# Two linear-attention stages: where queries and outputs are transposed, and when the next batch's q and k are made

## The reference

```
# layer 0: 16 heads of 8, causal linear attention
h = layernorm(x) * (1 + ca) + sa
q, k, v = split(h @ w_attn);  q = elu(q) + 1;  k = elu(k) + 1
S_t = S_(t-1) + k_t v_t^T;  z_t = z_(t-1) + k_t
y_t = (q_t S_t) / (q_t z_t + 1e-6);  x = x + ga * (y @ w_proj)
# layer 1: retention, the same sums with a decay per head
q, k = rope(h @ Wq.T), rope(h @ Wk.T);  v = h @ Wv.T
out = ((q k^T * scale) * decay_causal) v
out = groupnorm_per_head(out) * gn_w + gn_b
x = x + ga * ((silu(h @ Wg.T) * out) @ Wo.T)
```

## Time and profile before

| | us |
|---|---|
| median of 3 runs (1055.17 to 1057.34) | 1056.55 |
| the profiled execution | 1054.64 |
| its span, first to last instruction | 1052.8 |
| TensorE busy in the span | 860.5 (82%) |
| VectorE busy | 829.7 (79%) |
| GpSimd busy | 711.0 (68%) |
| ScalarE busy | 609.6 (58%) |

### The profile page before, as it was taken

How to read it: one execution, slowest core, us unless ns; L and a number is a source line. 1 busy time by engine, 2 the same in 40 slices (tenths; PEclk the granted TensorE clock), 3 DMA queues, 4 the chain that set the end, 5 groups by cost and what they waited for, 6 DMA issues and landing times. The chain is left out here.

```text
span 1052.8 us, 24355 instructions
## 1 busy us (share of the span) xinstructions
PE 860.5 (82%) x5240; PEld 622.6 (59%) x5240; DVE 829.7 (79%) x2581; ACT 609.6 (58%) x1524; POOL 711.0 (68%) x450
## 2 busy tenths in 40 slices
PE   5699999999968977888898988639888731999993
PEld 5456666666645754555555655426656521999993
DVE  5468888888875994888888888767988770899995
ACT  2545555555427965565656566347765212999992
POOL 4478878878853535999999999645599562255554
PEclk9799999999987998999999999859999855999997
DMA  8520000000000000000000000064566654544420
GB/s 243 165 66 2 0 0 0 0 0 0 0 1 5 0 1 1 11 11 20 10 20 10 20 10 20 21 184 109 149 207 208 192 193 143 159 131 134 133 68 20
DMA packets 64934, 70.11 MB, mean 67 GB/s; under 512 B 8965, under 2 KB 52178, under 8 KB 64740
## 3 DMA queue, kind: packets, MB, share of 16 engines
q1 hardware_dynamic: 50612, 47.20, 16.2%
q0 software_dynamic: 6368, 16.89, 4.7%
q10 hardware_dynamic: 7872, 5.08, 1.7%
HBM read 32.32 MB, written 24.50 MB: 54 GB/s over the span
## 5 line engine op out<-in xcount | busy, mean ns | idle before, releaser
L475 POOL TENSOR_TENSOR a_kv<-a_qk,a_vv 128x2304 f32<-128x2304 f32 (+1 forms) x64 | 252.0, 3938 | 37.1 <-DVE a_qk L446 32.6
L485 PE MATMUL a_pS<-a_kv,utri 128*128 128x360 f32 (+3 forms) x768 | 259.7, 475 | 10.7 <-POOL a_kv L475 10.7
L574 DVE TENSOR_TENSOR a_tt<-a_pS,a_qk 128x360 f32<-128x360 f32 (+3 forms) x384 | 201.5, 527 | 75.4 <-PE a_pS L485 75.2
L485 PEld LDWEIGHTS a_pS<-a_kv,utri 128*128 128x128 f32 x768 | 140.5, 191 | 96.2 <-issue 29.8
L591 POOL TENSOR_TENSOR a_tt<-a_tt 128x1152 f32<-128x1152 f32 (+1 forms) x64 | 144.7, 2260 | 37.7 <-DVE a_tt L574 37.6
L2016 POOL DMA_INDIRECT out_dram<-x_o,x_place x71 | 69.1, 974 | 76.1 <-DVE x_o L2003 75.1
L602 DVE TENSOR_REDUCE a_nd<-a_tt 128x144 f32<-128x720 f32 (+3 forms) x128 | 104.3, 817 | 1.0 <-POOL a_tt L591 0.9
L538 ACT ACTIVATE a_tt<-a_pI 128x144 f32<-128x144 f32 (+1 forms) x96 | 39.8, 415 | 96.0 <-PE a_pI L493 95.9
L1596 POOL DMA_INDIRECT ys<-m_S,m_dest x64 | 63.0, 984 | 35.2 <-issue 12.7
L546 ACT ACTIVATE a_qT<-a_pQ 128x128 f32<-128x128 f32 x96 | 26.5, 276 | 98.9 <-PE a_pQ L410 83.3
L1954 PE MATMUL x_pZ<-w,x_hT 128*128 x568 | 75.9, 277 | 1.4 <-issue 1.4
(11 more groups left out here) (299 smaller groups left out, 2103.4 us busy)
## 6 DMA issues: line engine op xcount, KB each, us to landing
x_yl<-ys SPq DMA_DIRECT2D x71, 193.5 KB, 2.4
X<-xs SPq DMA_DIRECT2D x16, 256.0 KB, 5.3
kx<-m_kc SPq DMA_DIRECT2D x64, 64.0 KB
ax<-m_pc SPq DMA_DIRECT2D x64, 64.0 KB
m_S<-X SPq DMA_DIRECT2D x16, 256.0 KB, 3.6
xs<-X SPq DMA_DIRECT2D x15, 256.0 KB
w<-in_L_ffn_W_dram SPq DMA_DIRECT2D x1, 2048.0 KB
m_S<-gw ACTq DMA_DIRECT2D x6, 256.0 KB, 2.9
```

Of the source, the lines that this page charges most:

```text
L475: pool.tensor_tensor(kv[:, t:t + 2, :, :, :].rearrange("p t h j i -> p (t h) j i"), kk.unsqueeze(2).to_broadcast([P, 2 * H, J, D]), rows.u ...
L485: pe.matmul(pS[c][:, 0:(h1 - h0) * SC], K.utri[:, :], flat[:, h0 * SC:h1 * SC], start=True, stop=True).then_inc(u_done, 1)
L574: v.tensor_tensor(tt[:, t, h0:h1, :, 0:D], pS[c][:, 0:(h1 - h0) * SC].rearrange("p (h j i) -> p h j i", i=D, j=J), q[:, h0:h1, :].unsqueez ...
```

## The change

1. The q transpose moves from pQ into bank pI, between the inter product and y's transposes. It no longer waits for pQ, but for every reader of pI: the inter copy, the q copy, the y copy.
2. TensorE's step: qkv of ta comes right behind the state sum, ahead of the projection; in layer 0 y is transposed one tile at a time, the first ahead of the q transpose in the middle of the step and the second at the step's end; in layer 1 both at the step's end. The second q transpose stands behind them, at the very end.
3. VectorE's step: q and k of the next batch's even tile (L446, L452 to L457) move ahead of the odd tile's products; the residual moves behind the state.
4. ScalarE's step: the copies out of qkv come ahead of the q copy, and normalise moves behind them, to the end of its half of the step; the second y copy stands behind it, and in layer 1 the gate behind that.
5. GpSimd's step in layer 1: the gate product is done a step later, ahead of rope and kv.

The ScalarE order at the end of layer 0's odd step in the loop, before: `a_yT` is the copy of y, `a_tt` the inter copy, `a_xn` normalise, `a_vv`, `a_ea`, `a_eb` the three operations behind a qkv, and the branch closes the loop.

Normalise and the y copy, which was in the odd step, now stand between the q copy and the gate. The diff, cut to the operations that move:

```diff
@@ places in PSUM and the q transpose
-        YT = H * J
-        QT = 3 * P
+        QT = H * J
+        YT = QT + P
         def pe_transpose_q(pe, b, t):
-            pe.wait_ge(v_ready, m)
             pe.wait_ge(qk_ready, qk_count(b, t))
-            pe.wait_ge(qk_free, m)
+            wait(pe, inter_ready, 3 * b + t - 1)
             wait(pe, qT_ready, 3 * b + t - 1)
-            pe.transpose(pQ[:, QT:QT + P], qk[:, 0, t, :], K.ident[:, :]).then_inc(q_T, 1)
+            wait(pe, yT_read, y_issued(b, t - 1))
+            pe.transpose(pI[:, QT:QT + P], qk[:, 0, t, :], K.ident[:, :]).then_inc(q_T, 1)
@@ pe_step
-            if out:
-                pe_project(pe, *out)
             if cur:
                 if ta > 0:
                     pe_inter(pe, b, ta)
                 pe_state_sum(pe, b, ta)
-                pe_transpose_q(pe, b, ta + 1)
                 if known(b, 1):
                     pe_qkv(pe, b + 1, ta)
-            if back:
-                pe_transpose_y(pe, back, b, u)
+            if out:
+                pe_project(pe, *out)
+            if cur and layer == 1 and u == 0 and known(b, 1):
+                pe_gate(pe, b + 1)
+            if back and layer == 0:
+                pe_transpose_y(pe, back, b, ta)
             if cur:
+                pe_transpose_q(pe, b, ta + 1)
                 pe_states(pe, b, tb)
                 pe_inter(pe, b, tb)
                 if tb < 3:
                     pe_state_sum(pe, b, tb)
-                    pe_transpose_q(pe, b, tb + 1)
                 if known(b, 1):
                     pe_qkv(pe, b + 1, tb)
                 if u == 1 and known(b, 2):
                     pe_transpose_x(pe, b + 2)
+            if back:
+                pe_transpose_y(pe, back, b, tb)
+            if cur and tb < 3:
+                pe_transpose_q(pe, b, tb + 1)
@@ act_step, second half
             if cur:
                 act_inter(act, b, tb)
-                if more:
-                    act_normalise(act, b + 2, tb)
             if layer == 1 and last:
                 act_sd(act, *last)
             if cur:
+                if known(b, 1):
+                    act_qkv(act, b + 1, tb)
                 if tb < 3:
                     act_qT(act, b, tb + 1)
-                if known(b, 1):
-                    act_qkv(act, b + 1, tb)
-                if layer == 1 and u == 0 and known(b, 1):
-                    act_gate(act, b + 1, (phase + 1) % 3)
+            if more:
+                act_normalise(act, b + 2, tb)
+            if back:
+                act_yT(act, *back, 1)
+            if cur and layer == 1 and u == 0 and known(b, 1):
+                act_gate(act, b + 1, (phase + 1) % 3)
@@ vec_step
-            if out:
-                vec_residual(v, *out)
             if cur:
                 vec_product(v, b, ta, 2)
...
             if cur:
                 vec_state(v, b, ta)
+            if out:
+                vec_residual(v, *out)
             if last:
                 vec_sum(v, last[0], 2 * last[1] + 1)
+            if cur and known(b, 1):
+                vec_qk(v, b + 1, ta)
             if cur:
                 vec_product(v, b, tb, 0)
...
                 vec_product(v, b, tb, 1)
-                if known(b, 1):
-                    vec_qk(v, b + 1, ta)
@@ pool_step
             if last:
                 pool_halve(pool, *last)
+            if layer == 1 and out:
+                pool_gate(pool, *out, (phase + (u - 3) // 2) % 3)
             if ahead:
                 if layer == 1:
                     pool_rope(pool, *ahead)
                 pool_kv(pool, *ahead)
-            if layer == 1 and back:
-                pool_gate(pool, *back, (phase - 1) % 3)
```

More of the change, by code:

```diff
@@ L486, in pe_states, with y_issued @@
                           start=True, stop=True).then_inc(u_done, 1)
+        def y_issued(b, t):
+            return 4 * b + t - 4 if layer == 0 else 2 * b + t // 2 - 2
         def pe_inter(pe, b, t):
@@ L491, in pe_inter @@
             pe.wait_ge(r_ready, 3 * b + t)
-            wait(pe, yT_read, 2 * b + t // 2 - (1 if t % 2 else 2))
+            wait(pe, yT_read, y_issued(b, t))
             pe.matmul(pI[:, 0:H * J], qT[:, :], R[:, :, :].rearrange("p h j -> p (h j)"),
@@ L503, in pe_transpose_q, with evacuated, pe_transpose_y @@
         def pe_transpose_q(pe, b, t):
-            m = 4 * b + 4 + t - 1
-            if isinstance(b, int):
-                m = min(m, NT)
-            pe.wait_ge(v_ready, m)
             pe.wait_ge(qk_ready, qk_count(b, t))
-            pe.wait_ge(qk_free, m)
+            wait(pe, inter_ready, 3 * b + t - 1)
             wait(pe, qT_ready, 3 * b + t - 1)
-            pe.transpose(pQ[:, QT:QT + P], qk[:, 0, t, :], K.ident[:, :]).then_inc(q_T, 1)
[L514 to L522, removed]
+            wait(pe, yT_read, y_issued(b, t - 1))
+            pe.transpose(pI[:, QT:QT + P], qk[:, 0, t, :], K.ident[:, :]).then_inc(q_T, 1)
+        def evacuated(pe, b, t):
+            wait(pe, inter_ready, min(3 * b + t, 3 * B) if isinstance(b, int) else 3 * b + t)
+            wait(pe, qT_ready, min(3 * b + t, 3 * B) if isinstance(b, int) else 3 * b + t)
+            wait(pe, yT_read, y_issued(b, t))
+        def pe_transpose_y(pe, at, b, t):
+            pe.wait_ge(y_ready, 2 * at[0] + at[1] + 1)
+            evacuated(pe, b, t)
+            if layer == 0:
+                pe.transpose(pI[:, YT:YT + P], y[:, t % 2, :], K.ident[:, :]).then_inc(y_T, 1)
+            else:
+                pe.transpose(pI[:, YT:YT + P], y[:, 0, :], K.ident[:, :])
+                pe.transpose(pI[:, YT + P:YT + 2 * P], y[:, 1, :], K.ident[:, :]).then_inc(y_T, 1)
         def pe_project(pe, b, u):
             n = 2 * b + u
-            pe.wait_ge(yT_ready, n + 1)
+            pe.wait_ge(yT_ready, 2 * n + 2 if layer == 0 else n + 1)
             wait(pe, x_done, n)
@@ L542, in act_qT, with act_yT @@
             act.wait_ge(q_T, 3 * b + t)
[L543 to L544 removed]
             wait(act, inter_ps, 3 * b + t - 1)
[L546 to L548 removed]
+            act.activation(qT[:, :], pI[:, QT:QT + P], ACT.Copy).then_inc(qT_ready, 1)
+        def act_yT(act, b, u, k=0):
             n = 2 * b + u
[L550 removed]
             if layer == 0:
+                act.wait_ge(y_T, 2 * n + k + 1)
                 wait(act, proj_ps, n)
[L553 removed]
+                act.activation(yT[:, k, :], pI[:, YT:YT + P], ACT.Copy).then_inc(yT_ready, 1)
             else:
+                act.wait_ge(y_T, n + 1)
                 wait(act, yT_ready, n)
@@ L642, in vec_y @@
             v.wait_ge(rec_done, n + 1)
-            wait(v, y_T, n)
+            wait(v, y_T, 2 * n if layer == 0 else n)
             v.tensor_tensor(y[:, :, :].rearrange("p t (h j) -> p (t h) j", h=H),
@@ L674, in pe_step @@
             cur, back, out = pair(b, u, 0), pair(b, u, -2), pair(b, u, -3)
-            if cur and not first:
-                pe_states(pe, b, ta)
-            if out:
-                pe_project(pe, *out)
             if cur:
+                if not first:
+                    pe_states(pe, b, ta)
                 if ta > 0:
@@ L708, in act_step @@
                     act_inter(act, b, ta)
-                if more:
-                    act_normalise(act, b + 2, ta)
-                act_qT(act, b, ta + 1)
                 if known(b, 1):
                     act_qkv(act, b + 1, ta)
-            if back:
-                act_yT(act, *back)
+                act_qT(act, b, ta + 1)
+            if back and layer == 0:
+                act_yT(act, *back, 0)
+            if more:
+                act_normalise(act, b + 2, ta)
             if layer == 1 and last:
@@ L761, in vec_step @@
                 vec_product(v, b, tb, 1)
-                if known(b, 1):
-                    vec_qk(v, b + 1, ta)
+            if layer == 0 and done:
+                vec_stats(v, *done, 1)
             if last:
@@ L768, in vec_step @@
                     vec_var(v, *last)
-            if layer == 0 and done:
-                vec_stats(v, *done, 1)
             if cur:
@@ L780, in pool_step @@
         def pool_step(pool, b, u, phase):
-            last, back, ahead = pair(b, u, -1), pair(b, u, -2), pair(b, u, 1)
+            last, out, ahead = pair(b, u, -1), pair(b, u, -3), pair(b, u, 1)
             if last:
                 pool_halve(pool, *last)
+            if layer == 1 and out:
+                pool_gate(pool, *out, (phase + (u - 3) // 2) % 3)
             if ahead:
@@ L885, in _ @@
                             pool_step(pool, 3 * i + 2 + k, 1, 2 + k)
-                for b in range(B - 2, B + 1):
+                for b in range(B - 2, B + 2):
                     for u in range(2):
```

3 lines of the change are left out of this document (removed).

## The result

The changed kernel takes 1076.36 us, median of 4 runs (1072.17 to 1077.61); the kernel before takes 1056.3 beside it, median of 4 (1055.17 to 1057.34). The ratio is 1.0183, 95% interval 1.0153 to 1.0213: slower, as forecast, by 20 us in place of 30. The profiled execution after is the fastest of its four, 1072.17 with a span of 1070.4, so spans differ by 17.6 us. What lies around the two attentions changed by 0.1 or less in all, in parts that cancel: +0.3 ahead of layer 0's first states, -1.6 between the layers, +1.2 behind layer 1's last.

A forecast was written before the change was run, and what follows sets the result against it. No engine is full, so a ring of waits, with TensorE in it twice, sets the pace. 14 batches at +1.45 (layer 0) and +0.9 (layer 1), less about 1 a layer, give +31: 1086 us, range 1060 to 1108.

The forecast's parts named there:

- slower by normalise behind qkv: Layer 0's odd step: fourth x transpose waits for normalise, behind three operations on the last qkv; next states lose 1.65 us.
- layer 0: even step: Layer 0, from the even step's states to the odd step's: 7.41 us plus 0.5 issue, 7.9, against 8.08 before.
- layer 1: qkv to states, over the gate: Layer 1, even step's odd-tile qkv to next states: q transpose waits for the inter copy, 6.75 us against 5.46 before.
- a sign of being wrong: In either layer, states that start right behind kv would show the forecast wrong; kv was to end before TensorE asks.
- Issue in the even step: Layer 0: transposes carry up to four waits, behind which TensorE issues slowly; 0.5 us a step, bounds 0 and 0.8.
- The q copy ahead of the gate: Layer 1, ScalarE: q copy waits for a q transpose behind two y transposes, 1.6 to 1.85 us after the qkv.
- The gate term: Layer 1: later inter copy behind the gate holds the q transpose ahead of the states; loss 1.3 us, bounds 0.85 and 1.6.
- The count of 14 batches: Both layers: x transposes happen in 14 batches each, 14 x 1.45 and 14 x 0.9; last two gain about 1 a layer.
- the loop's end: Close of a loop pass, no longer issued ahead: 0.6 us in layer 0 with waits ahead of y, 0.5 in layer 1.
- The last step of the sum: Whole kernel: +31 on the profiled 1054.64 gives 1085.6; runs' median lies 0.2% above that execution, so 1086 us.
- no change: Rival for the whole kernel: PE's work is the same and issue costs vanish, 1052 to 1063 us; chance 0.13.
- Faster: Rival, both layers: fourth x transpose met by kv anyway, states 0.1 us behind kv, 1034 us; chance 0.08.

The follow-up runs named there:

- the first experiment: Changed kernel with normalise of the odd tile put back behind the inter copy, ahead of the qkv copies, in both steps: 1038.86 us, ratio to before 0.9835.
- the last experiment: Layer 0 of the changed kernel with normalise early and projection ahead of qkv; layer 1 of the kernel before with early even-tile q and k: 1025.34 us.
- the third: Changed kernel with VectorE's q and k of the even tile back behind the odd tile's products: 1118.21 us, ratio 1.0588.
- the sixth: Kernel before with only normalise of the odd tile moved behind the copies out of qkv: 1108.05 us, ratio 1.0502.

## Why the prediction was right, and where its sizes were off

The forecast, slower by normalise behind qkv, is shown from both sides: taking that place out of the changed kernel removes the loss, putting it into the kernel before makes one. In clean batches the two halves add up: late normalise alone costs 1.77 / 1.61 us, early q and k alone gain 0.72 / 1.09; together +1.05 / +0.52, and the change measured +1.08 / +0.46. So, if the two halves add up inside the change as well, the other moves came to about nothing together with normalise late. With normalise early they cost something: the first experiment's batch is 0.47 / 0.37 longer than that of early q and k alone (15.75 - 15.28, 16.32 - 15.95). In layer 0 the projection's place, 0.73, is more than that; the transposes' moves were not run by themselves.

| step of the prediction, us | forecast | measured |
|---|---|---|
| layer 0: even step | 7.9 | 7.70 (212.80 - 205.10) |
| states to the last qkv | 6.35 | 6.31 |
| fourth x transpose behind that qkv | 2.4 | 2.28 |
| next states behind that transpose | 0.85 | 0.81 |
| batch | 17.5 | 17.08 |
| layer 1: qkv to states, over the gate | 6.75 | 6.35 (518.44 - 512.09) |
| states to the last qkv | 1.94 | 2.04 |
| that qkv to the next states | 2.5 | 2.52 |
| those to the next such qkv | 6.8 | 6.67 |
| batch | 17.9 | 17.5 |

Each step is there and in its order: the last transpose waits for `a_xn`, and a q transpose waits for the inter copy behind the gate. In layer 0's loop kv is done 0.73 to 2.5 us ahead of the states, as forecast. In layer 1 it is done 1.7 us ahead of the even step's states, but the odd step's start right behind it, which I had listed as a sign of being wrong. kv came when I had put it (7.77 after the even step's states; 530.76 - 523.00 = 7.76), and TensorE was ready for the odd states ahead of the 8.2 that I gave it: they start 0.39 us behind the q transpose at 512.98, against 0.16 at 518.28, so kv held them for about 0.2 us. This does not show in the time, since the next q transpose waits 1.20 us for the gate all the same. Three sizes made +31 of what was +17.6 in spans.

- *Issue in the even step.* I took 0.5 a step; the even step is 0.29 over the 7.41 without issue. With 0.2 too much in the odd step, most of it in ScalarE's chain (its v copy comes 0.84 behind the qkv, 219.95 - 219.11, where I had 0.92), layer 0's batch was put 0.38 too long: 14 x 0.38 = 5.3.
- *The q copy ahead of the gate.* I put the q copy at 1.6 to 1.85 after the qkv, with 0.3 of issue in it. The q transpose starts 0.92 after its qkv (530.59 - 529.67) and the copy 1.22 (513.31 - 512.09). The gate term is then close to the low bound of 0.85 that I gave it, +0.89 in place of +1.3, which with the other terms is 14 x 0.43 = 6.0.
- *The count of 14 batches.* In layer 0 the first two batches lost 0.25 us together, in place of 2.1; in layer 1 0.90, as two batches further on do. The clock is in these numbers too: over the first batch of layer 0 it was granted at 0.83 before and 0.88 after, over that of layer 1 at 1.00 and 0.91, so what the change alone did to the first batches is not shown. The last distance, from the first states of the last batch but one to those of the last, gave back 1.06 in layer 0 and 1.12 in layer 1, about as forecast.

The larger errors in the steps, 0.2 in the even step and 0.3 at the q copy, are issue time that I charged and that the rows do not show in full; at the loop's end, where I charged most, it was right. The last step of the sum also has a slip: 1085.6 and 0.2% more are 1087.5, not 1086.

Of the rivals, "no change" missed by 20 us, though TensorE's work in a batch of layer 0 rose by only 0.1 (15.18 to 15.28). The Trainium skill, Perfetto Trace Analysis, Identifying the Most-Contended Engine, has one optimise the engine of highest occupancy first, and judge TensorE's headroom by MFU (its share of the peak rate) and weight-load time, not by matmul time. By weight loads TensorE was busy for 9.77 of the 16.02 us of a layer 0 batch before. Orders of the same work ran here from 1025 to 1118 us, so which engine is busiest did not tell what a move would do. In the last experiment's layer 0 TensorE's two figures are 98% for matmuls and 64% for weight loads (109.22 of 170). "Faster" needed ScalarE's chain to end with kv. It fell to that chain. Where the first experiment moves normalise out of it, the time is 1038.86, near this rival's 1034, but not by its mechanism in layer 0: kv ends there 1.15 us ahead of the even step's states and 0.73 ahead of the odd step's, not 0.1. A suspect that came up with the trace after was VectorE's wait for the y transposes at a step's end, 1.5 us at most, the first of these entries in the wait list of layer 0; the other two are TensorE's wait for normalise (us in all, times, longest):

```profile
DVE a_y L649 <- PE a_pI L525: 16.1, 11, 1.5
PEld a_pT L388 <- ACT a_xn L380: 15.2, 11, 1.4
PE a_pT L388 <- ACT a_xn L380: 12.6, 11, 1.1
```

In the first experiment, which leaves y's transposes where they are, the first is down to 0.2 us in all and the other two are gone: it was a consequence.

## What to carry to other kernels

Before moving an operation behind others on an in-order engine, ask what its new predecessors wait for: normalise did not get longer, it got behind three operations on the last product of a loop pass (the last qkv). When a change is made of several moves, price each alone in both kernels; here one call of VectorE alone gained 26 us, more than the change without its loss did (1038.86, 16 us less than the kernel before beside it), and one of ScalarE cost more than the loss. Issue time seen ahead of one instruction that waits is no price for every instruction with waits.

## What the runs showed of the hardware that I had not expected

A wait can be followed by more than its own length, when TensorE's clock is lower behind it. In the third and sixth experiments some batches of layer 0 had the states behind the 1.15 us wait 1.4 to 1.6 us longer. In the third, the rows show 0.58 granted for those 3.47 us and 0.99 over the whole next batch, whose states follow the same 1.15 us wait; in the sixth, 0.55 was granted for the 3.67 us behind 232.60. The changed kernel has that wait in every batch of layer 0, and its clock stays at 1.00 there from the second batch on. The Trainium skill, TensorE: Matmul & The Clock Gate, What's actually happening, has the clock follow how busy TensorE was recently. The rows agree with that only in part. The two kernels whose clock fell have longer batches in layer 0 than the changed kernel (17.8 to 19.5 us against 17.1), but their layer 1, with batches of 18.97 and 18.65 us, stayed at 1.00 over its long middle (450 to 650 and 450 to 640 us of their spans). What tips the clock is not settled by these runs.
